# New orders for the first and last sequences of a decoder layer, and five weights on ScalarE's DMA queue

## The reference

```python
x = x + attn(layernorm(x))            # RWKV-like: r, k, v, gate from mixes of x[t] and x[t-1]
x = x + xattn(layernorm(x), ctx, ctx) # 32 query heads over 8 key/value heads of the context
x = x + ffn(layernorm(x))             # layernorm, quantised W1, gelu, quantised W2, residual

# attn, per head of 16 channels, chunks of 64 tokens with a state:
att = rr @ kk * Wm                    # Wm: decays below, bonus on the diagonal
y = att @ vv + rr @ state * wb
y = groupnorm(y) * g;  return y @ Wo.T + bo
# ffn: mx_quant rounds blocks of 32 to 8 bits with a shared power of two,
# of the weights too
h = mx_linear(mx_layernorm(x), W1, b1);  h = mx_linear(mx_gelu(h), W2, b2)
```

## Time and profile before

| | |
|---|---|
| time, three runs | 1353.01, 1359.17, 1360.65 us; median 1359.17 |
| span of the profiled execution (first to last instruction) | 1355.6 us, 3.6 under the median of the runs |
| PE busy | 1249.7 us (92%) |
| VectorE busy | 1134.3 us (84%) |
| ScalarE busy | 823.1 us (61%) |
| POOL busy | 636.6 us (47%) |
| moved by DMA | 97.09 MB, of it 37.16 MB read from HBM |

### The profile page before, as it was taken

How to read it: one execution, slowest core, us unless ns; L and a number is a source line. 1 busy time by engine, 2 the same in 40 slices (tenths; PEclk the granted TensorE clock), 3 DMA queues, 4 the chain that set the end, 5 groups by cost and what they waited for, 6 DMA issues and landing times.

```text
span 1355.6 us, 34643 instructions
## 1 busy us (share of the span) xinstructions
PE 1249.7 (92%) x13352; PEld 797.8 (59%) x13352; DVE 1134.3 (84%) x1960; ACT 823.1 (61%) x1577; POOL 636.6 (47%) x700
## 2 busy tenths in 40 slices
PE   1677989999999999999999999999999999999744
PEld 1564666656666666566666666666666666666411
DVE  5889978888888887888888888888888888888875
ACT  1334475766666666666666666667666666666641
POOL 3756444544445445544445455444445454443322
PEclk8789999999999999999999999999999999999976
DMA  9335312222222223222212233222212322221212
GB/s 323 101 95 136 67 39 73 70 71 57 51 57 61 63 67 70 70 70 49 56 50 64 65 70 70 71 70 50 56 52 64 63 71 69 70 59 38 67 49 51
DMA packets 137332, 97.09 MB, mean 72 GB/s; under 512 B 108113, under 2 KB 110161, under 8 KB 136401
## 3 DMA queue, kind: packets, MB, share of 16 engines
q1 hardware_dynamic: 137168, 94.87, 27.8%
HBM read 37.16 MB, written 8.39 MB: 34 GB/s over the span
## 4 chain that ended last, share of the span: by engine, by line
PE 79%; DVE 10%; issue 4%; DMA 2%; POOL 2%; ACT 1%; SPq 1%; POOLq 0%; DVEq 0%; ACTq 0%
PE bank_b L547 15%; PE bank_y L599 8%; PE bank_a L547 8%; PE bank_y L663 7%; PE bank_a L537 7%; PE rt L566 5%; PE rt L614 4%; PE rt L627 4%; PE bank_o L633 4%; PE bank_b L654 4%; PE bank_a L654 4%; PE bank_o L593 2%; PE bank_y L585 2%; PE bank_y L580 1%; DVE negm L1614 1%
## 5 line engine op out<-in xcount | busy, mean ns | idle before, releaser
L3282 POOL TENSOR_TENSOR gmem<-gmem,unit_g 128x1024 bf16<-128x1024 bf16 x64 | 124.1, 1940 | 214.1 <-DVE unit_g L1667 214.1
L1614 DVE TENSOR_REDUCE negm<-rt 128x16 f32<-128x2048 f32 x64 | 146.2, 2284 | 2.3 <-PE rt L614 1.5
L663 PE MATMUL bank_y<-w2q,gmem 128*128 128x512 bf16 x512 | 122.4, 393 | 19.3 <-DMA gmem<-gmem 19.3
L2626 ACT ACTIVATE pT<-rt 128x2048 f32<-128x2048 f32 x64 | 120.0, 1875 | 28.1 <-PE rt L627 20.3
L547 PE MATMUL bank_a<-mix_r,w_Wr 128*128 128x128 f32 x1024 | 124.3, 280 | 5.6 <-POOL mix_r L3241 5.6
L547 PEld LDWEIGHTS bank_a<-mix_r,w_Wr 128*128 128x128 f32 x1024 | 118.5, 194 | 16.1 <-issue 10.1
L547 PE MATMUL bank_b<-mix_k,w_Wk 128*128 128x128 f32 x1024 | 122.1, 278 | 5.2 <-DVE mix_k L1560 5.2
L3273 POOL TENSOR_TENSOR gt<-gt,yT 128x512 f32<-128x512 f32 x32 | 41.1, 1285 | 181.0 <-ACT yT L2604 181.0
L547 PEld LDWEIGHTS bank_b<-mix_k,w_Wk 128*128 128x128 f32 x1024 | 120.5, 196 | 7.2 <-issue 7.2
L547 PE MATMUL bank_b<-mix_g,w_Wg 128*128 128x128 f32 x1024 | 122.0, 278 | 0.0
L547 PEld LDWEIGHTS bank_b<-mix_g,w_Wg 128*128 128x128 f32 x1024 | 118.6, 194 | 2.0 <-issue 1.6
(11 more groups left out here) (205 smaller groups left out, 2829.8 us busy)
## 6 DMA issues: line engine op xcount, KB each, us to landing
qx<-qdense SPq DMA_DIRECT2D x64, 224.0 KB, 3.1
context<-ctx SPq DMA_DIRECT2D x32, 384.0 KB, 3.3
xin<-x SPq DMA_DIRECT2D x32, 256.0 KB, 3.2
gmem<-w SPq DMA_DIRECT2D x16, 512.0 KB, 4.0
out<-x SPq DMA_DIRECT2D x32, 256.0 KB, 2.9
vp<-vz SPq DMA_DIRECT2D x32, 128.0 KB
odense<-oT SPq DMA_DIRECT2D x128, 32.0 KB, 1.9
pT<-Wv SPq DMA_DIRECT2D x1, 1024.0 KB, 8.1
```

The source lines that it names most:

```text
L663: done = e.matmul(bank_y[:, :], gqT[:, t, :], w2q[:, t, :], start=(t == 0), stop=(t == FT - 1))
L1614: e.tensor_reduce(negm[:, 0:H].rearrange("p (g a j) -> p g j a", g=4, a=2)[:, :, 2 * i:2 * i + 2, :], rt[:, :].rearrange("p (g j a s) -> p ...
L2626: e.activation(pT[:, :, :].rearrange("p g n -> p (g n)"), rt[:, :], ACT.Exp, scale=float(D) ** -0.5).then_inc(sem(f"act_ex{i}"), 1)
L3282: e.tensor_tensor(blocks(half), blocks(half), per_block(unit[f"g{i}"], 32), ALU.mult).then_inc(sem(f"pool_gsc{i}"), 1)
```

## The change

All five lists are reordered for the first sequences (up to about 8) and the last (from 27). The loops keep a repeated pattern of the same length but begin at other numbers: PE `range(7, 27)`, VectorE `range(9, 27)`, ScalarE `range(9, 28)`, POOL `range(8, 32)`, SP `range(10, 28)`. No instruction of arithmetic is added or removed; `project_out(0)` gets one more wait, for Wo. The number of table switches in the loop is the same.

SP's start, and the weights on ScalarE's own queue:

```diff
-            load_x(0)
-            load("masks", masks[:, :], masks_in)
-            load("columns", all_columns[:, :, :], columns)
-            load("heads", per_head[:, :], heads)
-            load_w12(0)
+            load("masks")
+            load("columns")
+            load_w12(0)
+            load("heads")
+            load_x(0)
             load_w12(1)
-            load("Wv", wv_rows, weights["Wv"])
-            load("b1", b1row[:, :], b1)
-            for k in ROWS:
-                load("rows", row[k][:, :], rows[k])
+            load_row("bo")
             load_x(1)
-            load("Wo", wt["Wo"][:, :, :], weights["Wo"])
-            load("Wg", wt["Wg"][:, :, :], weights["Wg"])
-            load("Wk", wt["Wk"][:, :, :], weights["Wk"])
-            load("Wr", wt["Wr"][:, :, :], weights["Wr"])
-            w12_turned(0)
             load_w12(2)
             load_w12(3)
             w12_turned(1)
+            w12_turned(0)
...
+            def load_weight(k):
+                dst = wv_rows if k == "Wv" else wt[k][:, :, :]
+                e.dma_start(dst, weights[k]).then_inc(sem(f"sp_{k}"), 16)
+
+            for k in ("Wo", "Wv", "Wk", "Wr", "Wg"):
+                load_weight(k)
             e.preload_act_table_set(TABLE_EXP)
```

ScalarE's loop:

```diff
                 e.preload_act_table_set(TABLE_GELU)
                 gelu(n - 4, 0)
                 gelu(n - 4, 1)
+                e.preload_act_table_set(TABLE_EXP)
                 out_odd(n - 3)
-                e.preload_act_table_set(TABLE_EXP)
                 rstd_log("x", n - 2)
                 rstd_exp("x", n - 2)
                 normalise_x(n - 2)
                 rstd_log("q", n)
                 rstd_exp("q", n)
+                e.preload_act_table_set(TABLE_GELU)
                 normalise_q(n)
                 queries_x(n - 2)
                 x_turned(n)
-                e.preload_act_table_set(TABLE_GELU)
                 gate_tanh(n - 1)
```

More of the change, by code:

```diff
@@ L193, in _, with load, load_row @@
         def _(e):
-            def load(name, dst, src):
+            once = {"masks": (masks[:, :], masks_in), "columns": (all_columns[:, :, :], columns),
+                    "heads": (per_head[:, :], heads), "Wv": (wv_rows, weights["Wv"]), "b1": (b1row[:, :], b1)}
+            for k in R_WEIGHTS[1:]:
+                once[k] = (wt[k][:, :, :], weights[k])
+            def load(name):
+                dst, src = once[name]
                 e.dma_start(dst, src).then_inc(sem(f"sp_{name}"), 16)
+            def load_row(k):
+                e.dma_start(row[k][:, :], rows[k]).then_inc(sem("sp_rows"), 16)
             def load_w12(n):
@@ L1105, in _ @@
+            for n in range(7, 27):
                 e.wait_ge(sem("dve_ze0"), n - 3)
@@ L1892, in _ @@
+            gelu_pow2(0, 0)
+            gate(3)
+            decayed(3, 1)
+            gelu_quantised(0, 1)
+            spread_v(4)
             stats_g(1)
+            scaled_y(3)
             norm_mv("g", 1)
-            decayed(3, 1)
-            mixed(4, "k")
+            gated_y(3)
             weighted(1)
-            gate(3)
+            gelu_round(0, 0)
             hidden(1)
-            gelu_round(0, 0)
-            gelu_max(0, 1)
+            gelu_quantised(0, 0)
             hidden_max(1)
@@ L1902, in _ @@
             hidden_pow2(1)
[L1903 removed]
+            first_sum(3)
             hidden_scale(1)
[L1905 removed]
+            stats_x(3)
             hidden_round(1)
[L1907 removed]
             hidden_quantised(1)
[L1909 to L1917 removed]
@@ L2242, in _ @@
             stats_g(25)
             norm_mv("g", 25)
+            gelu_round(24, 0)
+            gelu_quantised(24, 0)
             weighted(25)
+            gelu_max(24, 1)
+            scaled_y(27)
+            gated_y(27)
             hidden(25)
-            mixed(28, "v")
             hidden_max(25)
             hidden_pow2(25)
+            mixed(28, "v")
+            gelu_pow2(24, 1)
+            first_sum(27)
+            stats_x(27)
             hidden_scale(25)
+            norm_mv("x", 27)
@@ L2369, in _ @@
+            decayed(30, 1)
+            mixed(31, "v")
+            norm_mv("f", 28)
             gate(30)
-            decayed(30, 1)
+            gelu_max(27, 1)
             stats_g(28)
             norm_mv("g", 28)
+            gelu_pow2(27, 1)
             weighted(28)
             hidden(28)
-            mixed(31, "v")
+            scaled_y(30)
+            gated_y(30)
             hidden_max(28)
+            gelu_round(27, 1)
             hidden_pow2(28)
+            spread_v(31)
+            gelu_quantised(27, 1)
@@ L2378, in _ @@
+            first_sum(30)
             hidden_scale(28)
+            stats_x(30)
+            norm_mv("x", 30)
             hidden_round(28)
             hidden_quantised(28)
[L2381 to L2391 removed]
@@ new lines, in _ @@
+            rstd_exp("x", 4)
+            rstd_exp("q", 6)
+            e.preload_act_table_set(TABLE_GELU)
+            normalise_x(4)
+            out_odd(3)
+            queries_x(4)
+            normalise_q(6)
+            gelu(2, 1)
+            x_turned(6)
+            gelu(2, 0)
+            values_copied(5)
+            maxima_turned(4)
+            gate_tanh(5)
+            gelu(2, 3)
+            gate_in(5)
+            gelu(2, 2)
+            e.preload_act_table_set(TABLE_EXP)
+            squares(5)
```

2204 lines of the change are left out of this document (908 added, 1296 removed).

## The result

| | before | after |
|---|---|---|
| median of the runs | 1356.1 us | 1368.9 us |
| span of the profiled execution | 1355.6 us | 1366.4 us |
| PE busy | 1249.7 us | 1248.9 us |

The changed kernel is slower: the ratio is 1.010, 95% interval 1.007 to 1.014. The prediction, 1342 us with a range of 1326 to 1356, is wrong, in its sign too.

The account below looks back on a forecast made before the run. The middle was taken as PE-bound, with idle PE only at the ends. Start -19, loop +7.8 and tail -6 gave -17.2 on the 1355.6 us span: 1338.4; with 3.6 us from span to median, 1342 us, range 1326 to 1356.

Parts of the forecast that it names:

- The start: Up to x1(7): earlier project("r", 0) and x1(0) at 69 win 19 us, bounds 27 and 8.
- If the two queues share evenly: Start, SP's and ScalarE's DMA queues: 1.2 MB at 180 GB/s puts x(0) at 10 us, w12(1) at 13.
- if the five weights went first, at 20: Start, loads: x(0) would land at 20 us if ScalarE's five weights, 5 MB, went ahead of SP's queue.
- priced at +1: Start, x1(2) to x1(7): project_v(3), 3.6 us, moves in and 2.4 stay idle: 197.8, 1 us more.
- The prediction's own signs of being wrong: x1(0) over 75, VectorE idle before w12_scale for pieces in the first 40 us, or turn_x without idle and period unchanged.
- Rival (b): Start: the early start isn't kept, x(0) at 20 us, a head of 8, total 1353; chance 0.19.
- Rival (d): Start: the new queue changes nothing by itself, the gain is of the order; no time or chance of its own.
- The loop: Passes n = 9 to 27: moved gelu load makes the PE wait 0.41 us in each of 19, 7.8 us lost.
- qdense, also behind the load, is done about when turn_x ends and adds nothing: Loop, ScalarE: qdense behind the moved gelu load was taken to add nothing to the 0.41 us per pass.
- The upper bound, 15 us: Loop: most it was to lose, if scores_max waits as long again as turn_x; lower bound 0.
- The end: Tail: x1(31) 1.3 us earlier, down(31, 0) near 1341.5, 3 us more before gated_y(31); -6, bounds 0 and -12.
- Rival (c): Loop: load before normalise_q costs load and drain together, 1.8 us per pass, total 1368, slower; chance 0.05.

Follow-up runs that it names:

- weights_on_sync: Changed kernel with the loop's table loads back, the store ahead of queries_spread and the five weights on SP's queue behind x(1): 1335.7 us, ratio 0.985.
- after_weights_on_sync: Changed kernel with only the new queue undone, the five weights asked for on SP's queue behind x(1): 1359.2 us, ratio 1.004.
- new_start_old_end: Changed start with weights on SP's queue, loop loads as before, store ahead of queries_spread, the kernel before's order from sequence 24: 1335.4 us, ratio 0.987.
- after_loads_back: Changed kernel with ScalarE's two table loads of the loop (exp and gelu) put back where they were: 1350.2 us, ratio 0.998.
- before_loads_moved: Kernel before with only its loop's two table loads moved, exp ahead of out_odd and gelu ahead of normalise_q: 1372.2 us, ratio 1.014.
- end_only: Kernel before up to sequence 24 on all engines, then the changed kernel's end: 1358.3 us, ratio 1.003.
- start_only: Changed start up to sequence 11, weights on ScalarE's queue, then the kernel before's order, table loads included: 1349.8 us, ratio 0.996.

## Why the prediction was wrong

**The start: -10.9 instead of -19. Failed step: "If the two queues share evenly."** SP's queue got a quarter of the bytes, an eighth from 6 to 10 us (0.22 of 1.66 MB). x(0) came at 19.4 us, the bound that the prediction gave for "if the five weights went first, at 20", and x1(0) at 79.7. What stood behind that step held: with the weights behind x(0), the marks came out within 2 us, in weights_on_sync and in after_weights_on_sync (new_start_old_end is later for another reason, below). Two of its terms missed and made up for each other, which is luck: in weights_on_sync norm_mv("q", 0) ended at 14.9 us, not 17, and project("r", 0) came 12.6 us behind that, not 10.8. From x1(2) to x1(7), priced at +1, the changed kernel took 195.2 us, 1.8 less than before. The prediction's own signs of being wrong were there: x1(0) over 75, and VectorE idle for a piece (3.6 us at 13.5). Rival (b) had this case, x(0) at 20, with a head of 8 us, and missed by 3; it blamed the lateness on VectorE's work and on late pieces as much as on the queue. Rival (d), that the queue changes nothing by itself, is not right for this order: it costs 8 to 9 us.

**The loop: +19.2 instead of +7.8. The mechanism of the step held; what stood behind it on another queue was put at nothing.** Slack 0.90, load 1.28: 0.41 us per pass forecast, 0.46 measured at turn_x and 0.50 in the period. The failed sentence is "qdense, also behind the load, is done about when turn_x ends and adds nothing". For the PE that is so; for SP's queue it isn't: queries_spread waits for qdense, the store stands behind it, normalise_o waits for the store to land. normalise_o started 12.8 to 13.6 us into most passes before and 14.0 to 14.3 into the short ones after; from 14.8 on every pass of these two kernels is long. The border is not sharp: a pass of after_loads_back with 14.25 is long (39.3), one of before_loads_moved with 14.7 is not (38.8). Three passes of the kernel before were already beyond it. What carries a pass over it is a store that lands late, 4 to 5 us after its issue instead of 3; the pass in the prediction's rows is a short one. The upper bound, 15 us, was too low for the same reason.

**The end: +2.5 instead of -6. Failed step: the advances were added up as if the path behind them kept them.** Two of them can be read: first_sum(31) to the first up(31, ·) became 1.1 us shorter, not 3, and first_sum(31) itself came not 1.3 us earlier against x1(26) but 4.4 later. Over all traces that stretch costs 1.5 to 6 us more with the new end. Behind x1(31) the time runs through sequence 31's own cross-attention and feed-forward; taking down(30, ·) out of the way leaves the PE to wait 13.3 us for hidden_turned(31) where it waited 10.5 for gelu_turned(30, ·). So the size is shown and the cause stays open: which of the reordered calls between x1(26) and x1(31) makes the 3.6 us more of idle time was not tried; nor is it settled how the 2 to 7 us of end_only divide.

**Rival (c)**, the slower one, got the sign but not the cause: the load's successor starts 0.02 us behind its end (832.58 + 1.28, 833.88), so no drain is seen, here as in the earlier trace rows. The Trainium skill, page "ScalarE: Activation LUTs", section "What ACT_TABLE_LOAD costs", adds a drain of 1.38 us to each load; the trace disagrees, and the measurement decides. The average pass lost 0.5 us to the load itself and as much by way of the store.

By these stages -10.9 + 19.2 + 2.5 = +10.8 us, the difference of the spans. Undone one by one in the changed kernel, the gelu load gives back 18 us and the queue 10; with both loads and the queue undone and the store first it is 20 us faster than the kernel before. Of the 3.6 us that the prediction put on the span 1.8 are there in every run; the other 1.8 came from a median of three runs that lay 3 us above the later medians.

## What to carry to other kernels

When an instruction is delayed on one engine, follow everything that waits for it, DMA issues included, and then what is queued behind those issues on the same queue and who waits for that landing: here one moved line on ScalarE came back through a store. A second DMA queue takes bandwidth from the first by packets; ask for what is needed first on it alone, and for large transfers behind it. A period of a loop is not enough to judge it by: count the passes that are longer, since they show which chain has almost no slack left. A transfer that something waits for needs slack for its slow cases too: the same store took 2.0 us to land in one place of the queue, 3.1 in another, and up to 5 now and then.

## What was not expected of the hardware

VectorE and POOL can hold each other up. In weights_on_sync VectorE's bf16 rounding started 0.2 us ahead of POOL's product, which then took 3.72 us. In four kernels the rounding starts 0.2 us ahead of this product, and in those four it takes 3.72; in all others, where it does not, 2.75 or 2.76:

```profile
39.89 1.30 DVE L1593 SCALAR_TENSOR_TENSOR hw<-gmem,pow_w 128x1024 bf16<-128x1024 f32 x1
```

```profile
40.09 3.72 POOL L3027 TENSOR_TENSOR att<-masks,per_head 128x1536 f32<-128x1536 f32 x1
```

In new_start_old_end pow_w, a call of 0.18 us, came 0.1 us behind the same product; the product took 2.76 us and VectorE's instruction 2.68:

```profile
40.00 2.76 POOL L5564 TENSOR_TENSOR att<-masks,per_head 128x1536 f32<-128x1536 f32 x1
```

```profile
40.10 2.68 DVE L2700 TENSOR_SCALAR pow_w<-amax_w 128x32 uint16<-128x32 uint16 x1
```

The product ends at 42.76 and the small call at 42.78. With the calls behind it, stretched too, x1(0) is 6.7 us later, from a piece that came 1.1 us later; in start_only the same calls are stretched (2.82 us for one of them at 48.84) and x1(0) is some 4 us later. Both kernels have the order of weights_on_sync or of the changed kernel up to there. hidden_quantised in the long passes meets a POOL product in the same way. The kernel before has such a meeting too, in its first 10 us:

```profile
6.04 2.76 POOL L3301 TENSOR_TENSOR att<-masks,per_head 128x1536 f32<-128x1536 f32 x1 [3.21 <-DMA per_head<-heads]
```

```profile
6.17 2.67 DVE L1772 TENSOR_SCALAR per_head<-per_head 128x48 f32<-128x48 f32 x1 [1.25 <-ACT per_head L2672]
```

In all four kernels with this start the small call begins within 0.2 us behind the product and takes 2.66 to 2.77 us. In seven of the others no POOL instruction runs then, and it takes 0.17 to 0.19; in the last three it begins 0.3 us behind a POOL product of 1.90 us and takes 1.6. Each time the two end within 0.1 us of each other.

The Trainium skill, page "SBUF — State Buffer", section "SBUF: two separate sides", says that the two engines share a pair of ports as a lock, held for the whole instruction by the one that starts first; on VectorE's side that goes for instructions in a two-port mode and, against a POOL instruction that reads SBUF, for those with two inputs there. These rows agree in that the later one does not end before the earlier one; which mode VectorE was in is not shown. No run moved one of the instructions to test it; the comparison is between kernels that differ in other things too.
